# The norm and transposes of a row made in the middle of the row ahead of it, and a first row that begins on a quarter megabyte of weights

## What is computed

```python
xn = layernorm(x)                                     # x: (4, 512, 256)
# attention branch: 16 heads of 128, 4 key/value heads, causal
Q, K, V = xn @ Wq + bq, xn @ Wk + bk, xn @ Wv + bv
ctx = softmax(Q K^T / sqrt(128) + mask) V
s = layernorm(xn + gelu(ctx @ Wo + bo)) * gamma + beta
# gate branch (FFN), hidden size 1024
gate, up = split(xn @ w_gate_up.T)
g = silu((silu(gate) * up) @ w_down.T)
out = x + s * g
```

## Time and profile before

| | |
|---|---|
| time, median of 3 runs | 725.94 us (725.47 to 728.41) |
| the profiled execution | time 726.24 us, span 724.3 us |
| busy: TensorE | 679.9 us, 94% |
| busy: VectorE | 489.8 us, 68% |
| busy: ScalarE | 429.3 us, 59% |
| busy: GpSimd | 280.7 us, 39% |
| mean granted TensorE clock | 0.987 |

### The profile page before, as it was taken

The page is one execution under the profiler, slowest core; times in us unless marked ns, Lnnn a source line. Parts: engine busy times, 40 slices in busy tenths (PEclk is TensorE's granted clock), DMA queues, the critical chain, the costliest instruction groups (busy, mean ns, idle before and its releaser), DMA issues.

```text
span 724.3 us, 13208 instructions
## 1 busy us (share of the span) xinstructions
PE 679.9 (94%) x4032; PEld 595.1 (82%) x4032; DVE 489.8 (68%) x1636; ACT 429.3 (59%) x1011; POOL 280.7 (39%) x328
## 2 busy tenths in 40 slices
PE   2889999999899999999899999999999999999993
PEld 1778888888788888898788888887888898888872
DVE  6764433335677777778768777776777778867777
ACT  3423232326666767677667676866667677767671
POOL 2599000001423324157615142583324157615234
PEclk9799999999999999999999999999999999999998
DMA  8343000002000000000200000002000000200000
GB/s 273 116 137 125 1 29 0 30 1 87 1 1 2 1 1 1 1 1 1 91 2 1 2 1 1 2 4 90 1 1 1 1 1 1 88 1 2 0 1 30
DMA packets 14522, 20.52 MB, mean 28 GB/s; under 512 B 752, under 2 KB 12144, under 8 KB 14192
## 3 DMA queue, kind: packets, MB, share of 16 engines
q1 hardware_dynamic: 13328, 14.37, 6.0%
q0 software_dynamic: 1120, 5.24, 2.2%
HBM read 15.41 MB, written 4.19 MB: 27 GB/s over the span
## 4 chain that ended last, share of the span: by engine, by line
PE 86%; DVE 6%; ACT 3%; issue 2%; DMA 1%; POOL 1%; SPq 0%; DVEq 0%; ACTq 0%
PE bank L941 29%; PE down_ps L941 28%; PE down_ps L1034 8%; PE down_ps L979 6%; PE bank L966 6%; PE bank L968 6%; PE bank L1021 2%; DVE cT_lo L808 2%; ACT cT_hi L690 2%; DVE hidT_lo L754 1%; DMA raw<-in_wgu 1%; PE bank L1000 1%; DVE xnT_lo L739 1%; POOL probs L551 1%; DVE pT_lo L792 1%
## 5 line engine op out<-in xcount | busy, mean ns | idle before, releaser
L551 POOL TENSOR_TENSOR probs<-probs,inv 128x512 f32<-128x512 f32 (+3 forms) x256 | 181.4, 723 | 391.3 <-DVE inv L892 391.3
L681 ACT ACTIVATE probs<-probs,least 128x512 f32<-128x512 f32 (+3 forms) x256 | 142.4, 558 | 46.5 <-DVE least L885 45.0
L885 DVE CUSTOM_DVE_ANT_0 probs<-bank,mask 128x512 f32<-128x512 f32 (+3 forms) x256 | 121.5, 487 | 12.6 <-issue 11.9
L687 ACT ACTIVATE pT_hi<-down_ps 128x512 fp32r<-128x512 f32 x156 | 92.8, 595 | 49.4 <-PE down_ps L1034 42.6
L792 DVE TENSOR_TENSOR pT_lo<-down_ps,pT_hi 128x512 fp32r<-128x512 f32 x156 | 107.0, 686 | 17.5 <-ACT pT_hi L687 14.3
L1034 PE MATMUL down_ps<-ident,probs 128*128 128x128 f32 x624 | 94.0, 273 | 2.3 <-POOL probs L551 2.3
L1034 PEld LDWEIGHTS down_ps<-ident,probs 128*128 128x128 f32 x624 | 75.9, 141 | 14.9 <-POOL probs L551 2.5
L941 PE MATMUL down_ps<-wo_lo,cT_hi 128*128 128x256 f32 x256 | 73.5, 287 | 4.1 <-DVE cT_lo L808 3.0
L803 DVE SCALAR_TENSOR_TENSOR qT_lo<-bank,bias,qT_hi 128x512 fp32r<-128x512 f32 x64 | 47.7, 749 | 41.2 <-ACT qT_hi L671 41.2
L941 PE MATMUL bank<-kT_lo,qT_hi 128*128 128x512 f32 (+2 forms) x192 | 70.6, 368 | 2.2 <-issue 2.2
L941 PE MATMUL down_ps<-wo_hi,cT_lo 128*128 128x256 f32 x256 | 72.1, 281 | 0.0
(11 more groups left out here) (142 smaller groups left out, 1566.4 us busy)
## 6 DMA issues: line engine op xcount, KB each, us to landing
x_row<-in_x SPq DMA_DIRECT2D x4, 512.0 KB, 6.9
raw<-in_wgu SPq DMA_DIRECT2D x4, 512.0 KB, 6.1
raw<-in_wq POOLq DMA_DIRECT2D x2, 1024.0 KB, 5.1
raw<-in_wo POOLq DMA_DIRECT2D x2, 1024.0 KB, 6.3
g_scratch<-g_out SPq DMA_DIRECT2D x4, 512.0 KB, 2.9
x_b<-in_x SPq DMA_DIRECT2D x4, 512.0 KB, 3.6
g_b<-g_scratch SPq DMA_DIRECT2D x4, 512.0 KB, 4.6
out<-res SPq DMA_DIRECT2D x3, 512.0 KB, 3.6
```

The costliest lines, as they stand in the source:

```text
L551: nc.gpsimd.tensor_tensor(p, p, inv[:, u % UNITS, g:g + 1].to_broadcast([P, (tile_of(u) + 1) * P]), ALU.mult).then_inc(probs_made, 1)
L681: nc.scalar.activation(p, p, ACT.Exp, bias=least[:, u % UNITS, g:g + 1], scale=-1.0, accum_out=total[:, u % UNITS, g:g + 1]).then_inc(exp_ ...
L687: nc.scalar.activation(hi[:], ps, ACT.Copy).then_inc(probsT_hi, 1)
L885: nc.vector.tensor_tensor_reduce(out=probs[t][:, g, :], in0=ps[:, 0:(t + 1) * P], in1=mask[:, (T - 1 - t) * P:], scale=-SCALE, scalar=BIG, ...
```

## The change

It reorders the beginning and moves the preparation of rows 1 to 3.

- SP loads row 0 as four tiles (128 KB each, one semaphore each), then the rest of the weights. ACT's queue loads the identity and a lead of two parts: 128 gate and 128 up columns for each half of the features, 256 KB in all, enough for `gate_up(0, 0)`. The FFN weights now have eight parts: lead 0 and 1, rest of the first half 2 and 3, `wd` 4 and 5, second half 6 and 7. DVE makes the low parts 0, 1, 3, 4; GpSimd 2, 5, 6, 7.
- PE starts with 14 dummy products of 512 columns over a zeroed tile `clock`, into a bank that is overwritten later.
- Row 0's normalised tiles are each transposed as they are made.
- For rows 1 to 3, in the row ahead: statistics behind `hid_low` of block 1, normalising behind that of block 3, transposes and split at block 5. `root1` for row 1 stands on GpSimd behind the FFN splits, those of rows 2 and 3 behind the split of part 10 (first half of `wq`) and part 13 (last of `wo`).
- `xT_ps` is now banks 2 and 3 of `down_ps`, and `down` writes its four tiles, two to a bank, into banks 0 and 1 (`down_out`). Rows of tokens share a smaller buffer, and SP loads rows 2 and 3 later.
- The attention weights are loaded by SP instead of GpSimd, ahead of the stores of `g_out`.
- ACT's and DVE's loops over rows 1 to 3 are written out.

```diff
+CLOCK_RUNS = 14
+TOKENS_AT = 5
+LEAD = 128
...
-    xT_ps = [flat[0:2], flat[2:4],
-             [down_ps[:, 0, :], down_ps[:, 1, :]], [down_ps[:, 2, :], down_ps[:, 3, :]]]
+    down_out = down_ps[:, 0:2, :].rearrange("p a (t d) -> p (a t) d", d=D)
+    xT_ps = [down_ps[:, 2, :], down_ps[:, 3, :]]
...
-    DVE_PARTS = (0, 4, 5)
-    POOL_PARTS = (1, 2, 3)
+    LEAD_PARTS = DC
+    DVE_PARTS = (0, 1, 3, 4)
+    POOL_PARTS = (2, 5, 6, 7)
+    ROOTS_AT = (10, 13)
...
-        load_tokens(0)
+        for t in range(T):
+            sp.dma_start(x_rows[:, (B - 2) * T + t, :], x_v[0][:, t, :]).then_inc(x_tile_in[t], 16)
+        load_piece(0, skip=LEAD_PARTS)
+        load_piece(1)
+        sp.sem_inc(g_free, 1)
         load_tokens(1)
-        sp.dma_start(ident[:], ident_in).then_inc(ident_loaded, 16)
-        load_piece(0)
-        load_tokens(2)
-        load_tokens(3)
-        load_piece(1)
...
-        sp.wait_ge(ffn_split_dve, 1)
+        sp.wait_ge(ffn_split_dve, 3)
         sp.wait_ge(ffn_split_pool, 1)
         load_piece(2)
...
+        sp.wait_ge(ffn_split_dve, len(DVE_PARTS))
+        sp.wait_ge(ffn_split_pool, 2)
+        load_attention(FFN_PIECES)
+        sp.wait_ge(ffn_split_pool, len(POOL_PARTS))
+        load_attention(FFN_PIECES + 1)
+        for k in range(FFN_PIECES + RAW_SLOTS, len(pieces)):
+            sp.wait_ge(attn_split, sum(len(p) for p in pieces[FFN_PIECES:k - RAW_SLOTS + 1]))
+            load_attention(k)
+
         for b in range(B):
             sp.wait_ge(g_made, b + 1)
             sp.dma_start(g_v[b], g_out[:]).then_inc(g_stored, 16)
...
         root1(0)
+        for part in POOL_PARTS:
+            ffn_low(part)
         root1(1)
...
+                if n in ROOTS_AT:
+                    root1(2 + ROOTS_AT.index(n))
...
+        act.dma_start(ident[:], ident_in).then_inc(ident_loaded, 16)
+        for src, at, _ in pieces[0][:LEAD_PARTS]:
+            act.dma_start(raw_view(0, at), src).then_inc(lead_in, 16)
...
+        def next_tokens(b, c):
+
+            if c == 1:
+                mean_and_variance(b + 1)
+            elif c == 3:
+                normalise(b + 1)
+            elif c == TOKENS_AT:
+                xT_low(b + 1)
...
             for c in range(1, FC):
                 gate_up(b, c, first)
-                if first and c == 1:
-                    transpose_tokens(2)
-                    transpose_tokens(3)
-                    pe.wait_ge(xT_split, B * DC)
+                if c == TOKENS_AT and not last:
+                    transpose_tokens(b + 1)
                 down(b, c - 1, first)
...
+        pe.wait_ge(clock_tile, 1)
+        for _ in range(CLOCK_RUNS):
+            nc.tensor.matmul(gate_ps[1], clock[:, 0:P], clock[:], start=True, stop=True)
         pe.wait_ge(ident_loaded, 16)
-        transpose_tokens(0)
-        transpose_tokens(1)
-        pe.wait_ge(xT_split, 2 * DC)
+        transpose_tokens(0, first=True)
+        pe.wait_ge(xT_split, DC)
         gate_up(0, 0, first=True)
```

More of the change, by code:

```diff
@@ L270, in build @@
     raw = [sb(f"raw{i}", [P, PIECE], F32, early) for i in range(RAW_SLOTS)]
+    x_rows = sb("x_rows", [P, (B - 1) * T, D], F32, early)
+    xn = sb("xn", [P, T, D], F32, early)
+    stats1 = sb("stats1", [P, T, 6], F32, early)
+    ve1 = sb("ve1", [P, T], F32, early)
     first = ExitStack()
[L273 to L276, removed]
+    clock = sb("clock", [P, L], F32R, first)
     first.close()
@@ L404, in parts, with landed @@
                 n += 1
-    def landed(eng, k):
+    def landed(eng, k, lead=False):
+        if lead:
+            eng.wait_ge(lead_in, 16 * LEAD_PARTS)
+            return
         loaded, start = (raw_in, 0) if k < FFN_PIECES else (attn_in, FFN_PIECES)
         eng.wait_ge(loaded[k % RAW_SLOTS], 16 * sum(
-            len(pieces[i]) for i in range(start, k + 1) if i % RAW_SLOTS == k % RAW_SLOTS))
+            len(pieces[i]) - (LEAD_PARTS if i == 0 else 0)
+            for i in range(start, k + 1) if i % RAW_SLOTS == k % RAW_SLOTS))
     banks, banks_last = ring(), ring(last=True)
@@ L480, in ffn_low, with root1 @@
                     nc.gpsimd.tensor_tensor(lo, raw_view(k, at), f32(hi), ALU.subtract).then_inc(ffn_split_pool, 1)
+        def root1(b):
+            pool.wait_ge(var_made, b + 1)
+            nc.gpsimd.tensor_tensor(norm[:, b * T:(b + 1) * T, 1], ve1[:], neghalf[:], ALU.pow).then_inc(rstd_made, 1)
         root1(0)
+        for part in POOL_PARTS:
+            ffn_low(part)
         root1(1)
[L484 to L499, removed]
         for n, k, at, (hi, lo) in parts():
@@ L628, in _, with ffn_row @@
             if c == 1:
-                ffn_high(4, 5)
-        with act.Fori(1, B) as b:
+                ffn_high(5)
+            if c == 2:
+                ffn_high(6, 7)
+            if c == TOKENS_AT:
+                xT_high(1)
+        def ffn_row(b, last=False):
             gate_part(b, 0)
@@ L638, in _ @@
                 hid_high(b, c)
+                if c == TOKENS_AT and not last:
+                    xT_high(b + 1)
+        for b in range(1, B):
+            ffn_row(b, last=b == B - 1)
         def gelu(b):
@@ L775, in _ @@
             hid_low(0, c)
-            if c == 1:
-                ffn_low(*DVE_PARTS[1:])
-        with dve.Fori(1, B) as b:
+            next_tokens(0, c)
+        for b in range(1, B):
             for c in range(FC):
@@ L943, in product, with transpose_tokens @@
             return ins
-        def transpose_tokens(b):
-            pe.wait_ge(xn_made, b + 1)
-            for c in range(DC):
-                for t in range(T):
-                    last = nc.tensor.transpose(xT_ps[b][c][:, t * P:(t + 1) * P],
-                                               xn[:, b % 2, t, c * P:(c + 1) * P], ident[:])
-                last.then_inc(xT_done, 1)
+        def transpose_tokens(b, first=False):
+            if not first:
+                pe.wait_ge(xn_made, b + T)
+                pe.wait_ge(xT_split, b * DC)
+            for t in range(T):
+                if first:
+                    pe.wait_ge(xn_made, t + 1)
+                for c in range(DC):
+                    last = nc.tensor.transpose(xT_ps[c][:, t * P:(t + 1) * P], xn[:, t, c * P:(c + 1) * P], ident[:])
+                    if t == T - 1:
+                        last.then_inc(xT_done, 1)
         def gate_up(b, c, first=False):
@@ L978, in down @@
                 for t in range(T):
-                    last = nc.tensor.matmul(down_ps[:, t, 0:D], hidT[c % 2][left][:, t * P:(t + 1) * P],
-                                            wd_s[right][:, c, :], start=c == 0 and n == 0,
-                                            stop=c == FC - 1 and n == len(PASSES) - 1)
+                    last = nc.tensor.matmul(down_out[:, t, :], hidT[c % 2][left][:, t * P:(t + 1) * P],
+                                            wd_s[right][:, c, :], start=c == 0 and n == 0 and t % 2 == 0,
+                                            stop=c == FC - 1 and n == len(PASSES) - 1, skip_group_check=True)
             return last
```

129 lines of the change are left out of this document (69 added, 60 removed).

## The result

The changed kernel takes 731.2 us (median of 5 runs, 729.91 to 732.48) against 725.53 of the kernel before in the same session: a ratio of 1.0066 with a 95% interval of 1.0036 to 1.0095. It is slower by some 5 us. I forecast 716.8 us with a range of 712.8 to 721.0 and gave slower a chance of 0.04. The profiled execution has a time of 731.2 and a span of 729.3.

What follows compares the result with a forecast made beforehand. TensorE, 86% of the chain, was taken as the bound, so only its idle, slow or removable work counts. An 11.8 us earlier first `down` less 2.7 in the FFN stage nets 9.1: 716.8 us, range 712.8 to 721.0.

Steps and rivals of the forecast that it cites:

- A rule against the row: Normalising of rows 1 to 3 beside GpSimd's long instructions: no double rate, 0.408 us a pass, so no wait.
- the held normalising: Part of a rival, chance 0.17: normalising waits behind a 1.9 us cast, `down(1,4)` some 2 us late; about 722 us.
- my sum: Rest of the FFN stage: 128.0 steady rhythm, 2.9 transposes, 2.2 waiting for weights, 4.1 on `hidT_lo`; 137.2 us.
- last tile of row 0 there: Start: the last of row 0's four token tiles lands at 5.2 us, bounds 4.3 and 5.7.
- first product: Start of the first `gate_up`: at 11.2 us instead of 17.8.
- clock at the first products: First `gate_up` products: a low TensorE clock costs 1.0 us, bounds 0 and 2.3, despite 14 dummy products.
- first `down`: Row 0's first `down` begins at 18.6 us instead of 30.38, a gain of 11.8.
- wait ahead of `gate_up(0, 4)`: Row 0: TensorE waits 2.2 us for second-half weights, both subtractions now being GpSimd's.
- TensorE waits on `hidT_lo`: FFN stage: GpSimd's attention-weight splits delay `hidT_lo`, costing TensorE 1.0, 0.7, 0 and 2.4, in sum 4.1 us.
- first `down` to first attention product: Rest of the FFN stage: takes 137.2 us, 2.7 more than the 134.5 before.
- normalising beside GpSimd: Rows 1 to 3: VectorE's normalising passes beside GpSimd's long instructions cost no wait.
- The rival "Slower": VectorE overruns in every row, nine blocks in all, 4.4 us slower, about 730; chance 0.04.

Runs made afterwards that it cites:

- the version with half passes: Changed kernel with the normalising of rows 1 to 3 made in eight passes of 128 columns instead of four of 256: 740.78 us, ratio 1.0191.
- The versions with the hold or ScalarE: Changed kernel with GpSimd waiting until the next row's normalising is done: 721.71 us; or with rows 1 to 3 normalised on ScalarE: 720.99 us.

## Why the prediction was wrong

**The step that failed** is the one under "A rule against the row": "nothing in it is read at double rate. From that I let it pass without a wait". I took the 0.408 us of a pass for its rate because the statistics of the same width take as long. A pass of 128 columns takes 0.332 at the least and one of 256 columns 0.406 (in the version with half passes): 0.58 ns for each further column, while VectorE's subtraction goes from 0.69 at 512 columns to 1.23 at 1024, 1.05 ns a column. Most of the 0.408 is fixed, and the rest runs at about double rate. So the rule that I had cited, of the Trainium skill ("GPSIMD Engine Reference", "1. Specifications"), applied: VectorE contends with GpSimd in a two-port mode too. The trace agrees now, with 7.10 and 13.11 us for 1.4 us of work. What the runs show is the wait and its size; that the mode is its reason rests on this slope, and no run turns the mode off.

**And its size was wrong even as a rival.** I priced the held normalising as one wait behind one cast of 1.9, and gave the case 0.17. Each pass is held anew, because GpSimd starts its next instruction as a pass ends (its subtraction at 76.63, the pass recorded to 76.70). Two casts and two subtractions, 2.38 + 4.58 + 1.95 + 4.49, make the 13. Beside that goes a cost that I had not listed: 8.6 us of idling took the clock to 0.50, and the 4.9 us that follow hold the transposes, a `down` and the first products at half speed, some 2.4 more. With the terms as measured my sum becomes 128.0 + 2.9 + 2.2 + 2.2 on `hidT_lo` + 9.8 on `xn` + 2.4 of clock = 147.5, of the measured 148.9; the other 1.4 is not assigned.

The other steps, one by one:

| step | predicted | measured |
|---|---|---|
| last tile of row 0 there | 5.2 | 6.0 |
| first product | 11.2 | 12.06 |
| clock at the first products | 1.0 us lost | 13 products at 0.43, 2.6 us lost |
| first `down` | 18.6 | 20.71 |
| wait ahead of `gate_up(0, 4)` | 2.2 | 2.2, released by `wgu_lo` |
| TensorE waits on `hidT_lo` | 4.1 | 2.2 |
| first `down` to first attention product | 137.2 | 148.9 |
| normalising beside GpSimd | 0 | TensorE idle 9.8, and the clock |

The start missed by 2 us: tile and clock, both a little beyond the bad ends of my bounds (5.7 for the tile, 2.3 us for the clock). I had argued the clock from idle stretches of 2.4 to 2.6; here 1.0 idle, eight transposes and 1.9 idle were enough to lose it, and the dummies went for nothing. The statistics did cost nothing. Two readings of mine were off without consequence: the first attention product by 0.16, and GpSimd's toll on `hidT_lo` in the kernel before, which I put at about 5 and which is 4.1 in its trace. The rival "Slower" had the right engine but the wrong place: VectorE did not overrun in every row, it overran twice where GpSimd was busy, and rows 2 and 3 ran clean, as forecast. That its price, about 730, lies near the measured 731.2 is coincidence.

With the passes kept clear, the forecast is roughly met. The versions with the hold or ScalarE are 0.75% and 0.84% faster, some 5.5 and 6 us against my 9.1. In their traces the stretch for which I had 137.2 takes 138.4 and 136.8, with 3.8 and 3.4 on `hidT_lo` for my 4.1 and 2.1 ahead of `gate_up(0, 4)` for my 2.2, so the other terms of that sum were right. What is missing is at the start: the first `down` at 21.0 and 21.1 instead of 18.6.

## What to carry to other kernels

Before a VectorE operation is moved, look at what GpSimd does in its new place: an operation that was free beside an idle GpSimd can cost a whole GpSimd instruction per pass beside a busy one, and its own duration in the old place doesn't show that. If the GpSimd work can't be moved, cut it into instructions shorter than the slack of what waits: here that one edit turned the change from 0.7% slower to 1.1% faster than the kernel before, of which 0.7% would have come without the change. Judge a double-rate mode by the slope between two widths, not by one duration.

## What the runs showed of the hardware

While both had such instructions ready, VectorE and GpSimd took turns, one for one: four passes with four GpSimd instructions (13.11 us), and of eight as many as GpSimd had instructions, six (13.88) and four (14.00). The cost grows when the work is cut finer on VectorE's side and shrinks when it is cut finer on GpSimd's. Cutting has a price on GpSimd: a subtraction takes 1.28 at 512 columns, 2.38 at 1024 and 4.5 at 2048, and all attention splits together 39.6 us instead of 34.1, partly because short instructions that start beside a VectorE operation wait too (subtractions of 1.62 to 1.75 among those of 1.28).

Not every VectorE operation was held. From the changed kernel:

```profile
23.08 1.40 DVE L746 BATCH_NORM_STATS2 stats<-x_rows 128x6 f32<-128x256 f32 x4
...
23.47 2.40 POOL L504 TENSOR_TENSOR wd_lo<-raw,wd_hi 128x1024 fp32r<-128x1024 f32 x1 [9.66 <-ACT wd_hi L605]
...
24.93 0.96 DVE L753 TENSOR_SCALAR ve<-norm 128x4 f32<-128x4 f32 x1
...
41.23 1.95 POOL L518 CAST wq_hi<-raw 128x2048 fp32r<-128x2048 f32 x1
41.35 0.68 DVE L781 TENSOR_TENSOR hid<-gate,bank 128x512 f32<-128x512 f32 x1
```

The statistics took 1.40 beside the subtraction, as at 64.24 with GpSimd idle. The addition of 4 columns behind them, a scalar operation like the normalising, took 0.96 instead of 0.17 and ended with the subtraction. `hid`, which reads one of its two inputs from a bank of PSUM, kept its 0.68 beside a cast, where `hidT_lo`, with both in SBUF, is held (4.93 in the version with holds).
